# Transposes as transpose instructions, bias rows in bfloat16, two row groups, and gate logits with the gate weights stationary

## The reference, cut to what matters

```python
h = relu(adj @ layernorm(x) @ gcn_w + gcn_b);  h = layernorm(h) * ln_g + ln_b
xz = h @ w_in;  xc, z = xz[:, :256], xz[:, 256:]
u = silu(causal_conv4(xc, conv_w) + conv_b);  dbc = u @ w_xp            # 8 + 16 + 16 columns
dt = softplus(dbc[:, :8] @ w_dt + b_dt);  B, C = dbc[:, 8:24], dbc[:, 24:]
# state of 256 x 16, row after row:  hst = exp(dt * A) * hst + dt * B * u;  ys = hst @ C
x = x + ((ys + u * D) * silu(z)) @ w_out
xn = layernorm(x);  H = gelu(xn @ W1 + b1)                              # 512 columns
probs = softmax(H @ Wg + bg);  e = argmax(probs)
x = x + probs[e] * (H @ Wd[e] + bd[e])
```

## Time and profile before

| | us |
|---|---|
| median of 3 runs | 1831.45 (1830.98 to 1836.17) |
| the profiled execution, its own time | 1837.63 |
| its span from the first to the last instruction | 1835.8 |
| PE busy | 1554.7 |
| DVE busy | 1536.0 |
| ACT busy | 877.1 |
| POOL busy | 875.3 |

### The profile page before, as it was taken

One profiled execution on the slowest core, in us unless ns is written; L12 is line 12 of the kernel. 1 busy time (PEld: TensorE's weight loads), 2 busy tenths in 40 slices (PEclk: granted clock), 3 DMA queues, 4 the chain that ended last, 5 costly groups with the idle time before them and its releaser, 6 DMA issues. The chain is left out here.

```text
span 1835.8 us, 16658 instructions
## 1 busy us (share of the span) xinstructions
PE 1554.7 (85%) x4572; PEld 789.5 (43%) x4572; DVE 1536.0 (84%) x2015; ACT 877.1 (48%) x1558; POOL 875.3 (48%) x466
## 2 busy tenths in 40 slices
PE   6989888988989989898999999998989893634676
PEld 2333333333435445453545445454535452422444
DVE  8066979898999998999898989899899999898621
ACT  3143454453537365655546463746465564634311
POOL 0023434444345464646455564646465655557621
PEclk9999999999898989999898989898998986655788
DMA  8778989999997868878696959697887864334320
GB/s 307 255 287 289 324 321 323 351 336 350 328 341 251 322 251 311 301 255 331 233 341 227 331 207 328 234 327 258 296 293 273 313 225 157 104 126 136 123 67 12
DMA packets 150816, 479.42 MB, mean 261 GB/s; under 512 B 18244, under 2 KB 32592, under 8 KB 150594
## 3 DMA queue, kind: packets, MB, share of 16 engines
q1 hardware_dynamic: 103842, 318.02, 48.4%
q10 hardware_dynamic: 38560, 139.48, 21.6%
q0 software_dynamic: 8320, 20.86, 3.4%
HBM read 448.20 MB, written 33.22 MB: 262 GB/s over the span
## 5 line engine op out<-in xcount | busy, mean ns | idle before, releaser
L1168 PE MATMUL ps_adj<-ring,nodes 128*128 128x512 f32 x2048 | 952.4, 613 | 73.3 <-DMA ring<-adj 49.1
L488 POOL TENSOR_TENSOR h_c<-hidden,bc_ring 128x1024 f32<-128x1024 f32 x256 | 600.7, 2346 | 845.1 <-DVE inject L1036 575.5
L963 DVE TENSOR_TENSOR_SCAN hidden<-decay,state,inject 128x512 f32<-128x512 f32 x512 | 627.6, 1267 | 62.5 <-ACT decay L577 37.3
L1168 PEld LDWEIGHTS ps_adj<-ring,nodes 128*128 128x128 f32 x2048 | 394.2, 197 | 596.1 <-issue 463.0
L1036 DVE TENSOR_TENSOR inject<-dtu_sb,bc_ring 128x1024 f32<-128x1024 f32 x256 | 314.3, 1228 | 49.4 <-DMA bc_ring<-bc_dram 41.2
L577 ACT ACTIVATE decay<-dt_sb,negA 128x512 f32<-128x512 f32 x512 | 339.3, 711 | 9.1 <-DVE dt_sb L990 7.1
L1006 DVE TENSOR_TENSOR y_sum<-y_sum,h_c 128x1024 f32<-128x1024 f32 x224 | 273.7, 1222 | 24.2 <-POOL h_c L488 21.0
L570 ACT COPY state<-hidden 128x2 f32<-128x2 f32 x255 | 48.8, 191 | 416.8 <-DVE hidden L963 414.6
L452 POOL DMA_INDIRECT out<-o_sb,out_at x68 | 93.6, 1377 | 71.7 <-DVE o_sb L868 58.7
L1103 PEld LDWEIGHTS ps_y<-wg_sb,H 128*128 128x128 f32 x512 | 97.6, 297 | 19.6 <-issue 16.2
L1103 PE MATMUL ps_y<-wg_sb,H 128*128 128x8 f32 x512 | 98.9, 335 | 2.5 <-ACT H L661 2.5
(11 more groups left out here) (201 smaller groups left out, 1373.0 us busy)
## 6 DMA issues: line engine op xcount, KB each, us to landing
ring<-adj SPq DMA_DIRECT2D x512, 512.0 KB
bc_ring<-bc_dram ACTq DMA_DIRECT2D x256, 512.0 KB
wd_ring<-wd_rows SPq DMA_DIRECT2D x64, 320.0 KB, 3.3
bins<-nodes SPq DMA_DIRECT2D x32, 516.0 KB, 9.1
nodes<-x_rows ACTq DMA_DIRECT2D x8, 512.0 KB, 11.8
x_tile<-x_rows SPq DMA_DIRECT2D x16, 256.0 KB, 8.5
wd_rows<-Wd SPq DMA_DIRECT2D x8, 256.0 KB
ring<-Wd SPq DMA_DIRECT2D x1, 2048.0 KB, 9.1
```

Source lines behind the costliest of these rows:

```text
L488: nc.gpsimd.tensor_tensor(h_c[:, s % 2], hidden[:, s % 2], over_halves(bc_ring[:, s % BC_RING, 1]), ALU.mult).then_inc(hc_ready, 1)
L963: scan = nc.vector.tensor_tensor_scan(hidden[:, s % 2, h], decay[:, s % 2, h], inject[:, h], state[:, h, s:s + 1], ALU.mult, ALU.add)
L1168: last = nc.tensor.matmul(ps_adj[:, 0], nodes[:, m], ring[:, g % RING, m % GROUP], start=(m == 0), stop=(m == J - 1))
```

## The change

`logits` is replaced by three steps. `logit_parts` (PE) makes four products, one for each quarter of the hidden features, with `wg_sb[:, k]` (128 x 32, eight columns of weights and 24 of zeros) as the stationary operand and `H[:, k]` (128 x 512) moving, each written to another group of 32 partitions of `ps_y`. `logit_columns` (ACT) copies the 128 x 512 result into `front_b`. `logits` (PE) turns it by four transposes into `ps_y`. DVE then sums the four quarters with `reduce_sum` and adds `bg` in an instruction of its own. In a body with front work `logit_parts` stands in slot 10, `logit_columns` at the end of slot 10 on ACT, behind `fetch_rows`, and `logits` in slot 11; in body 15 they stand in slots 8, 6 and 8, in the tail between the hidden quarters of batch 1.

The products with the identity become `nc.tensor.transpose`. The bias product of an expert takes three rows of bfloat16 instead of 128 of float32: `bd / 8` is split into three bfloat16 parts by DVE at the start of the program, written into the table by one transfer in body 4, and multiplied by three rows of `ones`. The table's row is 288 KB instead of 320 KB. The two products of `dt` now stand together in slot `f[9]`, the second with its operands on partitions 32 to 39, and both wait for `low_ready` and `rows_ready`.

```diff
         def _(sp):
             def small_weights():
...
+                sp.wait_ge(pad_ready, 1)
...
+                                 (H[0:EXPERTS, 0, 0:P], bd[0:EXPERTS, 0])):
...
+                    if s == 0 and i == 4:
+                        sp.wait_ge(table_in, 16 * 2 * EXPERTS)
+                        sp.wait_ge(part_step, 6)
+                        sp.dma_start(wd_rows.ap()[:, 0:3, 4 * P:],
+                                     bd_parts[:].bitcast(F32)).then_inc(part_in, 16)
                     if s == 7 and batch:
-                        sp.wait_ge(table_in, 16 * 2 * EXPERTS)
+                        sp.wait_ge(part_in, 16)
...
+            def logit_columns(c, front):
+                c.wait(part_logits, -1, 1)
+                if front:
+                    c.wait(hn_ready, 1, 1)
+                nc.scalar.copy(front_b[:], ps_y[:, 0]).then_inc(cols_ready, 1)
...
                     if front and s == f[1]:
                         c.wait(gcn_done, 1, 1)
+                        c.wait(logit_done, -2, 1)
...
-                        nc.scalar.copy(low_sb[:], ps_f[0:8, 0]).then_inc(low_ready, 1)
+                        nc.scalar.copy(low_sb[:], ps_f[0:40, 0]).then_inc(low_ready, 1)
...
                     fetch_rows(s)
+                    if ffn and s == (6 if fast else 10):
+                        logit_columns(c, front)
...
+            rest = H[0:EXPERTS, 0, 0:P]
+            nc.vector.tensor_scalar_mul(rest, rest, 1.0 / EXPERTS).then_inc(part_step, 1)
+            for n in range(3):
+                dve.wait_ge(part_step, 2 * n + 1)
+                nc.vector.tensor_copy(bd_parts[:, n], rest).then_inc(part_step, 1)
+                if n < 2:
+                    dve.wait_ge(part_step, 2 * n + 2)
+                    nc.vector.tensor_tensor(rest, rest, bd_parts[:, n], ALU.subtract).then_inc(part_step, 1)
...
-                nc.vector.tensor_tensor(logit[:], ps_y[:, 0, 0:BLOCKS * EXPERTS].rearrange(
-                    "p (b e) -> p b e", b=BLOCKS), over_blocks(vec("bg", 0, EXPERTS)), ALU.add
-                    ).then_inc(gate_step, 1)
+                quarters = ps_y[:, 0].rearrange("p (b k e) -> p b e k", b=BLOCKS, k=4)[:, :, 0:EXPERTS]
+                nc.vector.reduce_sum(logit[:], quarters, AX).then_inc(gate_step, 1)
                 c.wait(gate_step, -1, 1)
+                nc.vector.tensor_tensor(logit[:], logit[:], over_blocks(vec("bg", 0, EXPERTS)), ALU.add
+                                        ).then_inc(gate_step, 1)
...
             def transpose(rows, bank):
                 for j in range(PICKS):
-                    last = product(bank[:, j * P:(j + 1) * P], [(rows[:, j, 0:P], ident)])
+                    last = nc.tensor.transpose(bank[:, j * P:(j + 1) * P], rows[:, j, 0:P], ident)
...
-                            [(hid[:, k, j * P:(j + 1) * P], weights[:, j, k]) for k in range(4)]
-                            + [(mean, weights[:, j, 4])]).then_inc(by_done, 1)
+                            [(hid[:, k, j * P:(j + 1) * P], weights[:, j, k * P:(k + 1) * P]) for k in range(4)]
+                            + [(ones[0:3], weights[0:3, j, 4 * P:].bitcast(BF16))]).then_inc(by_done, 1)
...
+            def logit_parts():
+                for k in range(4):
+                    last = product(ps_y[P // 4 * k:P // 4 * (k + 1), 0], [(wg_sb[:, k], H[:, k])])
+                last.then_inc(part_logits, 1)
 
             def logits():
                 for b in range(BLOCKS):
-                    last = product(ps_y[:, 0, b * EXPERTS:(b + 1) * EXPERTS],
-                                   [(H[:, k, b * P:(b + 1) * P], wg_sb[:, k]) for k in range(4)])
+                    last = nc.tensor.transpose(ps_y[:, 0, b * P:(b + 1) * P], front_b[:, b * P:(b + 1) * P], ident)
                 last.then_inc(logit_done, 1)
...
-                        product(ps_f[:, 1], [(wdt_sb[:, 0], low_sb[:])]).then_inc(dt_done, 1)
+                        c.wait(rows_ready, 1, 1)
+                        for h in range(2):
+                            product(ps_f[:, 1 - h], [(wdt_sb[32 * h:32 * h + 8, h], low_sb[32 * h:32 * h + 8])]
+                                    ).then_inc(dt_done, 1)
```

More of the change, by code:

```diff
@@ L750, in _ @@
             gelu(1, (0, 1))
+            logit_columns(c, False)
             gelu(1, (2, 3))
-            c.wait(gate_step, -1, 3)
+            c.wait(gate_step, -1, 4)
             nc.scalar.activation(expo[:], logit[:], ACT.Exp).then_inc(expo_ready, 1)
@@ L1222, in body @@
                         transpose(got[:, p], ps_e[:, 0])
-                    if front and s == f[10]:
-                        c.wait(rows_ready, 1, 1)
-                        product(ps_f[:, 0], [(wdt_sb[:, 1], low_sb[:])]).then_inc(dt_done, 1)
-                    if ffn and s == (8 if fast else 10):
-                        c.wait(h_ready, -1, 4)
+                    if ffn and s == (8 if fast else 11):
+                        if fast:
+                            logit_parts_of(c)
+                        c.wait(cols_ready, -1, 1)
                         logits()
+                    if ffn and s == 10 and not fast:
+                        logit_parts_of(c)
                     if batch and s in (10, 12):
@@ L1241, in body @@
                     if ffn and not fast and s == 15:
-                        c.wait(gate_step, -1, 8)
+                        c.wait(gate_step, -1, 9)
                         rank()
@@ L1299, in _ @@
             pe.wait_ge(coef_ready, 1)
-            product(ps_y[0:BLOCKS * EXPERTS, 0, 0:P], [(cells(coef[:]), ident)]).then_inc(coef_t_done, 1)
+            nc.tensor.transpose(ps_y[0:BLOCKS * EXPERTS, 0, 0:P], cells(coef[:]), ident).then_inc(coef_t_done, 1)
             hidden_units(2, (2, 3))
```

62 lines of the change are left out of this document (36 added, 26 removed).

## The result

| | before | after |
|---|---|---|
| median in us (lowest to highest, 4 runs each) | 1831.2 (1811.9 to 1836.2) | 1776.1 (1772.1 to 1781.8) |
| ratio, 95% interval | | 0.972 (0.964 to 0.980) |
| the profiled execution | 1837.63, span 1835.8 | 1772.06, span 1770.3 |

The kernel is faster by 55 us. A later comparison of the same two kernels, on chip 14, gave 1792.4 against 1837.4, ratio 0.975 (0.972 to 0.979); on which chip the first one ran is not on record.

A forecast was written before the change was run, and what follows sets the result against it. DVE was taken as the bound, reached by PE through ACT's waits. Bodies 4 to 14 -24.9, start -0.9 and tail -6.0 sum to -31.8 us, from the median 1831.45 to 1799.7; range 1784 to 1824.

The forecast's parts named there:

- What bounds the kernel, and the place: Bodies 4 to 14: DVE bounds; PE's time reaches it through ACT's 5.44 us wait for hidden quarters in body 7.
- Bodies 4 to 14: Broadcast and decay waits of DVE shrink, less its new work: -20.0 - 4.2 - 5.2 + 4.5 = -24.9 us.
- I take half: Bodies 4 to 14: half of 8.3 us decay waits (4.2) and of 10.5 us remaining broadcast waits (5.2) go.
- `logit_parts` at five passes of the lower clock: Slot 10 of body 7: the eight passes overlap partly and take 4.5 us, ending near 879.0, bounds 876 to 882.
- DVE's new work: The reduction over quarters adds 0.3 us in each of 15 bodies with a gate, +4.5 us, hidden by nothing.
- Bodies 1 to 3: No batch there; ACT's new wait is a pure addition but leaves 2.4 us or more before the scan: nothing.
- Tail: After the bodies, PE is longest: transposes, bias products and logits save 6.0 us, bounds 1 to 10.
- B: Rival: in the bodies the waits only move, no gain there and the cost stays; 1829 us, chance 0.12.
- C: Rival: ACT held at the end of slot 10 makes DVE late for slot 12; +38, 1870 us, chance 0.06.
- D: Rival: all 38.8 us of waits go and a third of POOL's 15.4; -46.3, 1785 us, chance 0.14.
- E: Rival: PE's clock stays low for longer in the tail; 1811 us (worked out as 1808), chance 0.10 shared with the serial groups.
- the serial groups: Rival: column groups run one after the other, parts take eight passes; 1813 us, chance 0.10 shared with E.

The follow-up runs named there:

- A again: The kernel after the change, unchanged, run and profiled once more, on chip 14: 1792.4 us, ratio 0.975 to the kernel before.
- B again: The kernel before the change, unchanged, run and profiled once more: ratio 0.9998; 1837.4 us on chip 14.
- one column group: Kernel after, with the four logit products accumulated into one group of 32 partitions in place of four groups: 1797.9 us, ratio 0.981 to the kernel before.
- A: The kernel after the whole change, as first measured: median 1776.1 us, ratio 0.972 to the kernel before.
- B with transposes: Kernel before, with only the products with the identity replaced by transpose instructions: ratio 0.993 to the kernel before.
- the new logits alone: Kernel before, with only the new logits (four column groups, copy on ACT, four transposes, sum on DVE): ratio 0.981 to the kernel before.
- B: The kernel before the change, as first measured: median 1831.2 us.

## Why the prediction was wrong, step by step

The steps that failed are sizes: half of the waits behind ACT instead of nearly all, five passes at the lower clock for the parts, nothing for bodies 1 to 3, and a tail priced without the clock behind the logits. Some 10 us more came from the stall in the time that the forecast started from.

**What bounds the kernel, and the place: right.** DVE is the bound, and PE's time reached it through ACT's wait for the hidden quarters. Moving one block of products behind them, with no work saved, gave 26.5 us.

**Bodies 4 to 14: right in kind, too small.** Forecast 20.0 + 4.2 + 5.2 less 3.3 (the share of these eleven in DVE's 4.5): 26.1. Measured 33.0, and 31.1 for A again against B again. Two terms failed, and a third held:
- "I take half" of the decay waits (4.2) and of the other broadcast waits (5.2). Nearly all of these waits, with the 20.0, went: 38.8 to 2.8 us, and 6.8 in A again. My reason for half was that DVE comes earlier too. It does, but ACT gains more than my sum had: from the first `dt` product to the quarters I reckoned 879.0 - 871.19 = 7.8 us, and it is 2.64. ACT, for which I left no room at the quarters, has 4.6 us.
- `logit_parts` at five passes of the lower clock, 4.5 us. It took 0.99: the groups run all together, and at the full clock. I had the two-pass end as a bound and moved away from it, since no row before showed it. With 3.55 us in its place (one column group) bodies 4 to 14 took 1065.4, still 28.8 less than before and more than forecast, so this term alone doesn't explain the miss.
- DVE's new work held: the two instructions take 0.28 and 0.19 us as foreseen. DVE's busy time in these bodies rose by only 1.3 us against before (1014.1 to 1015.3). Against the kernel with transposes, pair and the old logits in slot 11, in which DVE waits as little as in A, it is 2.9 us more (1012.4 to 1015.3), near the 3.3 of the forecast. Why before shows some 1.7 us more busy time than that kernel for the same instructions stays open.

The `dt` pair was costed at three or four passes, "in place of two". It takes the time of one product, 1.06 us for four passes, and that edit, which my sum gave no gain of its own, gives 23.8 us alone.

**Bodies 1 to 3: wrong.** "Nothing", and 5 us came. The step looked at ACT's slack (the new wait, 11.3 us in three bodies, shows in no longer time) and not at PE, which is late there: before, ACT waits for it at `front_a` and `front_b` for 49.5 us, DVE behind ACT for 22. After, these are 38.5 and 17 us. The 5 us are a difference of means over eight and six profiles that spread by 8; that they come from PE's shorter logits is argued from these waits, and no run shows it by itself.

**Start: right**, in so far as its 0.9 us can't be seen in a spread of 7.

**Tail: forecast 6.0, measured 7.6** (113.5 to 105.9, both without the stall), but by other terms. The transposes, forecast at 3.2, give 5.6 (113.4 to 107.8, with the pair), and the granted clock of the tail goes from 0.88 to 0.91 with them. The logits, at 0.3, give 6.3 alone and 3.4 on top of the transposes (107.8 to 104.4). The bias, forecast at a gain of 2.5, costs 1.5 (104.4 to 105.9). What the logits' term missed is the clock. PE in the tail with the old logits (transposes and pair in), then after:

```profile
1687.59 3.63 PE L1103 MATMUL ps_y<-wg_sb,H 128*128 128x8 f32 x32
1691.08 3.66 PE L1103 MATMUL ps_e<-bt_sb,w_sb 128*128 128x512 f32 x4
1695.51 1.16 PE L1103 MATMUL ps_e<-wd_ring,H 128*128 128x128 f32 x8 [0.78 <-ACT H L729]
```

```profile
1685.49 1.06 PE L1137 MATMUL ps_y<-H,wg_sb 128*32 128x512 f32 x8
1687.27 0.66 PE L1188 MATMUL ps_y<-const_sb,front_b 128*128 128x128 f32 x4 [0.71 <-ACT front_b L574]
1687.76 1.88 PE L1137 MATMUL ps_e<-bt_sb,w_sb 128*128 128x512 f32 x4
1690.42 1.16 PE L1137 MATMUL ps_e<-wd_ring,H 128*128 128x128 f32 x8 [0.78 <-ACT H L749]
```

Parts, copy and transposes take 2.27 us for the old logits' 3.49; behind them the same two quarters take 1.9 us in place of 3.7. The clock granted was 1.00 in the old logits (1687.6 to 1691.0) and 0.56 behind them (1691.1 to 1695.0); after, it was 1.00 for all of 1685.4 to 1690.4. I had priced what was replaced and not what stands behind it.

**The stall: half right.** I called it nothing to expect of every run. In these profiles it goes with the chip, so the median of before that I started from, 1831.45, probably had it: before takes 1832.4 and 1837.4 on the chips with it, 1822.6 and 1820.8 on the chip without, where the kernels nearest to A take 1772.5 and 1773.8. Of the 55 us first measured some 45 are the change's. Chip 14 has both kernels, and its medians differ by 44.9; the stretches give 32 in bodies 4 to 14, 5 in bodies 1 to 3 and 7.6 in a tail without the stall. The two agree in the sum and not in every part, for on chip 14 the tail gains nothing. 45 is still 13 more than forecast, in the terms named above.

**The rivals.** B and C didn't occur (the waits went, ACT's new wait is not seen in a batch body). D (all 38.8 us, 1785) was the nearest; its third of POOL's waits didn't come, they grew by 2.4. E and the serial groups didn't occur either: the granted clock of the tail rose from 0.86 to 0.94, and the groups ran together. (E stands at 1811 in the list and at 1808 where it is worked out; 1808 is what the sum gives.) The rule of the Trainium skill, "TensorE: Matmul & The Clock Gate", PE-mode transpose, had the clock stay low for longer; the granted clock rose from 0.89 to 0.93 in bodies 4 to 14 and is 1.00 around the transposes of body 7. The Trainium skill, "TensorEngine Tiling (Array Packing)", Key Properties, was right where my sum left it: tiles work in parallel (0.99 us against 3.55). Its drain at a change of mode fits the pick, 1.25 us with three rows against 1.00, but no run separates that cause from others.

## What to carry to other kernels

- Where the bound engine waits behind a second engine that waits for a third, count what the third does ahead of that hand-over. Work there is worth its whole length until the pool is empty, and nothing after; edits that each empty it don't add up, and an order costs nothing to try.
- Price what follows the replaced instructions too: their clock can change with them.
- Before costing a stall or a stretch from one profile, take a second one; here one stall of 10 us goes with the chip and bodies 1 to 3 vary by 8 us with the same products in them.

## What the runs showed of the hardware

- The granted clock fell in the old logits though PE never stood still. In B with transposes PE has no idle time from 859.8 on (4.08 us of it ended there), and the granted clock goes from 0.91 ahead of the logits of body 7 to 0.60 in them and 0.50 behind them. Windows of that kernel, columns as in the earlier trace rows: adjacency, `dt` and transposes; logits; hidden quarters; adjacency.

```profile
863.40:870.20 6.80, 6.80 (x18) 2.60 (x16) 5.87 (x6) 6.02 (x11) 4.31 (x3) 0.91 0.68 218
870.20:876.00 5.80, 5.80 (x34) 5.80 (x33) 5.55 (x6) 3.86 (x8) 2.65 (x2) 0.60 0.63 240
876.00:879.50 3.50, 3.50 (x5) 1.44 (x6) 3.43 (x4) 2.14 (x4) 3.35 (x2) 0.50 0.00 0
879.50:889.00 9.50, 9.50 (x21) 4.24 (x20) 9.17 (x11) 8.67 (x15) 7.66 (x5) 0.89 0.64 210
```

  PE is busy for all of 870.2 to 879.5 at 0.60 and 0.50, and the quarters pay for it too. In the one-column-group kernel, whose eight passes of the parts stand in the same place, the granted clock was 1.00 from 852.9 to 858.1. The new parts don't always have it: behind an idle time of PE of 1.36 us the new logits alone ran at 0.50 (861.3 to 863.2). In B the clock was at 0.50 already in the transposes ahead of the logits (873.5 to 877.5), behind idle times of 1.96 and 1.14 us.
- Four products of float32 into four column groups take the time of one, 0.99 us for eight passes at the full clock and 1.86 at the lower one; two on two row groups take the time of one, 1.06 us for four.
- A transpose instruction of a 128 x 128 float32 block takes 0.11 to 0.15 us (0.44 and 0.59 for four in body 7 of A, at the full clock), the product with the identity 0.26 to 0.27 (1.05 to 1.08 for eight instructions).
- A bfloat16 product over three rows between float32 products over 128 makes a pick 0.25 us dearer than one over 128 rows.
- What the stall of the tail is stays open. ACT and DVE stand still for 4 to 16 us at the logits, and PE behind them, where the profile names no releaser, in all six profiles of chips 14 and 15 and in none of the seven of chip 1.
